# Layer two's projection: each head's reciprocal norm is copied over its 16 rows by DMA instead of by a matrix product

## The chip, the core and the metric

The kernel runs as one program on one core of a Trainium2 chip. The metric is the time of one execution on the device in microseconds (us). The engines named below are TensorE (PE; its weight loads are PEld), VectorE (DVE), ScalarE (ACT), GpSimd (POOL) and SyncE (SP), which here only issues DMA transfers and waits.

## The reference, cut to what matters

Two transformer-like layers run over 2 x 2048 tokens of width 256 with 16 heads of 16 columns. The change lies in layer two, between its layer norm and its attention:

```python
def _l2norm(t):
    n = jnp.sqrt(jnp.sum(t * t, axis=-1, keepdims=True))
    return t / jnp.maximum(n, EPS)
def heads(W):                      # x is the layer-normed input, (B, T, 256)
    y = jnp.einsum('btd,od->bto', x, W)
    return y.reshape(B, T, NUM_HEADS, HEAD_DIM).transpose(0, 2, 1, 3)
Q = _l2norm(heads(Wq))
K = _l2norm(heads(Wk))
V = heads(Wv)
cos_sim = jnp.clip(jnp.einsum('bhtd,bhsd->bhts', Q, K), -0.999, 0.999)
```

So every 16 values of a query or key head are multiplied by one number, the reciprocal of their norm. The attention that follows (an arccos, a 16th power, a normalised product with V), the output projection and a feed-forward branch are the same in both kernels.

## The kernel before

The program is a row of phases, each of them a block that all engines leave together: constants; then for each layer the weights, the layer norm, the projection, the attention and the output. The phase of this study is the projection of layer two (`projection_phase` with `L == 1`, prefix `p1`).

It works on 8 blocks (`TB`) of 512 tokens. The normed input `xTa` lies transposed (features on partitions). In a block there are four feature tiles `ft` of 128 rows, two of queries and two of keys; a tile holds 8 heads of 16 rows (`FH` = 8, `DH` = 16). For each block:

- PE computes the values of two 128-token tiles (L528), then for each `ft` the projection `psS[ft % 2]` (L547) and behind it the product `expand` of the block before (L537), then the other two tiles of values, then `norms` (L520). `norms` adds the squares of each head: the 8 sums of tile `ft` land on partitions 32*ft to 32*ft+7 of `psO[0]`.
- ACT copies the values out (L570), copies each projection to `proj` (L584) and squares it to `sq` (L586), and takes the reciprocal root of the norms, `n_sb` (L599).
- DVE limits that to `r_norm` (L657) and then, for each `ft`, waits for `expand`, multiplies `proj` by it (L660) and splits the result into three bf16 parts that sum to it (`split_parts`, L437 to L440).
- SP stores the three parts of each `ft` to `qk_parts` in device memory (L487, 384 KB, rows of 1 KB) and the block's values to `v_store` (L491). The whole of `xTa` goes to `xT_store` in one transfer of 4 MB at the phase's start (L483).

`expand` is what puts a head's number on its 16 rows: a product of `r_norm` (8 rows used of 32) with the constant 0/1 matrix `selT`.

What sets the order is semaphores. DVE's `r_norm` waits for L599, which waits for `norms`, the last product of its block. `parts` has two buffers, so the split of a tile waits until the store of the tile two before it has landed (`s_st`). `proj` has two buffers (`projs`), so ACT's copy waits for the splits of two blocks before. DVE and ACT run a loop of two blocks; PE's program is written out.

Layer one's projection (`L == 0`) has the same shape without `expand`. In it SP also stores the bf16 parts of the norms: per block four transfers of 24 KB to `norm_parts` (L496), each out of 8 partitions that begin at partition 0, 32, 64 or 96:

```python
for f in range(NQK):
    sp.dma_start(io["norm_parts"][:, f * FH:(f + 1) * FH, bass.ds(i * 512, 512)]
                 .rearrange("a p t -> p a t"), n_parts[f * NCOL:f * NCOL + FH]).then_inc(s_nst, 16)
```

Of the kernel before, what the change touches and what calls it, by code (L numbers as in the profile page):

```python
# [13 lines left out]
F32 = mybir.dt.float32  # L14
BF16 = mybir.dt.bfloat16
ALU = mybir.AluOpType
# [36 lines left out]
class Mem:  # L53


    def __init__(self, nc, ctx):
# [28 lines left out]
        self.sels = self.q_stack[1][:, :].bitcast(F32)[:, 0:P + NCOL]  # L85
# [74 lines left out]
def load_projection(sp, m, io, L, loaded):  # L160

    vg_w = 2 * D if L == 0 else D
    sp.dma_start(m.wqk, io[f"wqk{L}"].rearrange("(k p) n -> p k n", p=P)).then_inc(loaded, 16)
    sp.dma_start(m.wvg[:, 0:KD * vg_w].rearrange("p (k n) -> p k n", k=KD),
                 io[f"wvg{L}"].rearrange("(k p) n -> p k n", p=P)).then_inc(loaded, 16)
    sp.dma_start(m.sels[:, 0:NCOL], io["sel"]).then_inc(loaded, 16)
    sp.dma_start(m.sels[:, NCOL:NCOL + P], io["selT"]).then_inc(loaded, 16)
    return 64
# [274 lines left out]
def projection_phase(nc, m, io, L):  # L443
# [3 lines left out]
    pre = f"p{L}"  # L447
    xTa = m.area(2 * NT * D, KD, B * T)
    vg_w = 2 * D if L == 0 else D
# [6 lines left out]
    selT = m.sels[:, NCOL:NCOL + P]  # L456
# [8 lines left out]
    r_norm = m.area(11520, 512)  # L465
    n_loads = 2
    with ExitStack() as ctx:
        (s_load, s_dve, s_bias, s_bias_row, s_proj, s_P, s_sq, s_nm, s_nsb, s_nparts, s_nst, s_vps, s_vfree, s_rn,
         s_e, s_efree, s_parts, s_v) = sems(
            nc, ctx, pre, "load", "dve", "bias", "bias_rows", "proj", "projected", "squared", "norm_mm", "norm_copied",  # L470
            "norm_parts", "norm_stored", "v_ready", "v_free", "rnorm", "expanded", "expand_free", "parts",
            "values")
        s_st = sems(nc, ctx, pre, "stored0", "stored1")
        s_xT, s_vst, s_ones = sems(nc, ctx, pre, "xT_stored", "values_stored", "stack_ones")
# [3 lines left out]
        def _(sp):  # L478
            if L == 0:
                sp.dma_start(bqk, io["bqk"]).then_inc(s_load, 16)  # L480
                sp.dma_start(bvg[0:1, :], io["bvg"]).then_inc(s_load, 16)
            if L == 1:
                sp.dma_start(io["xT_store"], xTa).then_inc(s_xT, 16)  # L483
            with sp.Fori(0, TB) as i:
                for ft in range(NQK):
                    sp.wait_ge(s_parts, 4 * i + ft + 9)
                    sp.dma_start(io["qk_parts"][:, ft * P:(ft + 1) * P, bass.ds(i * 512, 512)]  # L487
                                 .rearrange("a p t -> p a t"), parts[ft % 2]).then_inc(s_st[ft % 2], 16)
                if L == 1:
                    sp.wait_ge(s_vfree, 4 * i + 6)  # L490
                    sp.dma_start(io["v_store"][:, bass.ds(4 * i, 4), :], m.values[:, bass.ds(4 * i, 4), :])\  # L491
                        .then_inc(s_vst, 16)
                if L == 0:
                    sp.wait_ge(s_nparts, i + 2)
                    for f in range(NQK):
                        sp.dma_start(io["norm_parts"][:, f * FH:(f + 1) * FH, bass.ds(i * 512, 512)]  # L496
                                     .rearrange("a p t -> p a t"), n_parts[f * NCOL:f * NCOL + FH]).then_inc(s_nst, 16)
            for x in s_st:
                sp.wait_ge(x, 16 * (2 * TB + 1))
            if L == 1:  # L500
                sp.wait_ge(s_xT, 16)
                sp.wait_ge(s_vst, 16 * TB)
            if L == 0:
                sp.wait_ge(s_nst, 16 * (NQK * TB + 1))

        @block.tensor
        def _(pe):
            pe.sem_inc(s_nm, 1)
            if L == 0:
                pe.wait_ge(s_load, 16 * n_loads)  # L510
                nc.tensor.matmul(m.psM[0][:, :], m.ones_row[0:1, :], bvg[0:1, :], start=True, stop=True)\
                    .then_inc(s_bias_row, 1)
                pe.wait_ge(s_bias, 2)
# [18 lines left out]
            def expand(i, ft):  # L532

                pe.wait_ge(s_rn, i + 2)
                pe.wait_ge(s_efree, 4 * i + ft + 1)
                rows = slice(ft * NCOL, (ft + 1) * NCOL)
                nc.tensor.matmul(m.psS[ft % 2][:, 512:1024], selT[rows, :], r_norm[rows, :], start=True, stop=True)\  # L537
                    .then_inc(s_e, 1)


            for i in range(TB):
                if L == 1:
                    values(i, range(2))
                for ft in range(NQK):
# [5 lines left out]
                    if L == 0:  # L550
                        values(i, (ft,))
                    elif i > 0:
                        expand(i - 1, ft)
                if L == 1:
                    values(i, (2, 3))
                norms(i)
            if L == 1:
                for ft in range(NQK):
                    expand(TB - 1, ft)

        @block.scalar
        def _(act):
            act.sem_inc(s_P, 2)
            act.sem_inc(s_nsb, 1)
            if L == 0:
                act.wait_ge(s_bias, 2)
            def act_block(i, proj):
                def value_tile(tt):
                    act.wait_ge(s_vps, 4 * i + tt + 1)
                    nc.scalar.activation(m.values[:, bass.ds(4 * i + tt, 1), :], m.psM[tt % 2][:, 0:D].unsqueeze(1),  # L570
                                         ACT.Copy).then_inc(s_vfree, 1)

                if L == 1:
                    for tt in range(2):
                        value_tile(tt)
                act.wait_ge(s_nm, i + 1)
                for ft in range(NQK):
                    act.wait_ge(s_proj, 4 * i + ft + 1)
                    act.wait_ge(s_parts, 4 * i + ft + 1)
                    if L == 0:  # L580
                        nc.scalar.activation(proj[:, ft, :], m.psS[ft % 2][:, 0:512], ACT.Identity,
                                             bias=bqk[:, ft:ft + 1], scale=-2.0 if ft < 2 else 1.0).then_inc(s_P, 1)
                    else:
                        nc.scalar.activation(proj[:, ft, :], m.psS[ft % 2][:, 0:512], ACT.Copy).then_inc(s_P, 1)  # L584
                    act.wait_ge(s_P, 4 * i + ft + 3)
                    nc.scalar.activation(sq[:, ft, :], proj[:, ft, :], ACT.Square,  # L586
                                         scale=0.5 if L == 0 and ft < 2 else 1.0).then_inc(s_sq, 1)
                if L == 1:
                    value_tile(2)
                    value_tile(3)  # L590
                act.wait_ge(s_nm, i + 2)
                if L == 0:
                    act.wait_ge(s_nparts, i + 1)
                else:
                    act.wait_ge(s_rn, i + 1)
                if L == 0:
                    nc.scalar.activation(n_sb, m.psO[0][:, :], ACT.Copy).then_inc(s_nsb, 1)
                else:
                    nc.scalar.activation(n_sb, m.psO[0][:, :], ACT.Abs_reciprocal_sqrt, bias=ZERO_SHIFT)\  # L599
                        .then_inc(s_nsb, 1)  # L600
# [6 lines left out]
        def _(dve):  # L607
            dve.sem_inc(s_parts, 8)
            dve.sem_inc(s_vfree, 2)
            dve.sem_inc(s_efree, 2)  # L610
            dve.sem_inc(s_nparts, 1)
            dve.sem_inc(s_rn, 1)
# [3 lines left out]
            per_block = NQK * 3 + (3 if L == 0 else 0)  # L616
            chain_n = [0]
            if L == 0:
                dve.wait_ge(s_load, 16 * n_loads)
                nc.vector.tensor_scalar(bqk[:, 0:2], bqk[:, 0:2], -2.0, None, ALU.mult).then_inc(s_bias, 1)  # L620
                dve.wait_ge(s_bias_row, 1)
                nc.vector.tensor_copy(bvg_all, m.psM[0][:, :]).then_inc(s_bias, 1)
                dve.wait_ge(s_bias, 2)
            def dve_block(i, proj):
# [21 lines left out]
                if L == 0:  # L646
                    for ft in range(NQK):
                        dve.wait_ge(s_P, 4 * i + ft + 3)
                        split(ft)
                        value_tile(ft)  # L650
                    dve.wait_ge(s_nsb, i + 2)
                    dve.wait_ge(s_nst, 16 * NQK * i + 16)
                    split_parts(nc, link, n_sb, n_parts, n_rest).then_inc(s_nparts, 1)
                else:
                    dve.wait_ge(s_nsb, i + 2)

                    nc.vector.tensor_scalar(r_norm, n_sb, 1.0 / NORM_EPS, None, ALU.min).then_inc(s_rn, 1)  # L657
                    for ft in range(NQK):
                        dve.wait_ge(s_e, 4 * i + ft + 1)
                        nc.vector.tensor_tensor(proj[:, ft, :], m.psS[ft % 2][:, 512:1024], proj[:, ft, :], ALU.mult)\  # L660
                            .then_inc(s_efree, 1)
                        dve.wait_ge(s_efree, 4 * i + ft + 3)
                        split(ft)
# [5 lines left out]
        if L == 0:  # L669
            @block.gpsimd  # L670
            def _(pool):
                pool.wait_ge(s_proj, NQK * TB)
                pool.wait_ge(s_vps, NQK * TB)
                pool.wait_ge(s_nm, TB + 1)
                for stack in m.q_stack + m.k_stack:
                    nc.gpsimd.memset(stack[ROWS:P, :], 1.0).then_inc(s_ones, 1)
                pool.wait_ge(s_ones, 2 * B)
# [725 lines left out]
def program(nc, ins, out):  # L1403
    with ExitStack() as ctx:
# [11 lines left out]
        for L in range(2):  # L1416
# [4 lines left out]
            projection_phase(nc, m, mine, L)  # L1421
            if L == 0:
                distance_phase(nc, m, mine)
            else:
                cosine_phase(nc, m, mine)
# [3 lines left out]
def layout(inputs):  # L1429
# [21 lines left out]
        "ident": np.eye(P, dtype=np.float32), "sel": sel, "selT": np.tile(sel.T, (NQK, 1)),  # L1451
# [16 lines left out]
```

## Time and profile before

| | us |
|---|---|
| median of 3 runs | 7010.25 (7005.66 to 7014.32) |
| the profiled execution | 7006.62 |
| its span, first to last instruction | 7004.8 |
| layer two's projection in it, from PE's first product to DVE's last split | 2554.8 to 2698.9 |

The profile is one execution. "Busy" is the time in which an engine executes; the granted clock of PE is given as a share of full speed; the share of DMA is the mean busy share of the core's 16 DMA engines. A row of a timeline gives the start, the length, the engine, the source line and what was written from what; in brackets stands how long the engine had been idle and what ended that. SPq is the queue on which SyncE issues transfers.

### The profile page before, as it was taken

The page shows a single profiled execution, that of the slowest core. Times are in us where ns is not written, and L with a number is a line of the kernel's source. Part 1 is how long each engine was busy: PE and PEld are TensorE (multiplying, and loading weights), DVE is VectorE, ACT ScalarE, POOL GpSimd, SP SyncE. Part 2 cuts the span into 40 slices and gives each one's busy share as a digit, 9 for nine tenths or more (in the row PEclk, how much of TensorE's full clock was granted, in tenths as well). Part 3 has the DMA queues.
Part 4 walks back from the last instruction along what each step waited for, and adds up shares of the span by engine and source line. Part 5 has one row for each costly group of instructions (what it writes and reads, how often), then busy time and mean ns, then how long its engine had stood idle before and what let it go on. Part 6 is the DMA issues. An engine that isn't in the chain of part 4 may idle for free. (4 is left out here: it accounts for less than half of the span.)

```text
span 7004.8 us, 55795 instructions
## 1 busy us (share of the span) xinstructions
PE 4109.5 (59%) x17200; PEld 1398.6 (20%) x17200; DVE 6627.5 (95%) x6134; ACT 6429.7 (92%) x3748; POOL 3427.1 (49%) x1422
## 2 busy tenths in 40 slices
PE   5677777776777675454554554554544555544555
PEld 3222222222222242021111111111211111111212
DVE  7899999999999967999999999999999999999995
ACT  3699999999999935999999999999999999999995
POOL 0244444444444401565655656556565555656553
PEclk8988888889898887555556555565655555565657
DMA  3100000000000042000000000000000000000002
GB/s 130 55 16 12 15 12 16 11 16 14 13 15 12 10 148 72 6 15 8 15 8 9 8 15 8 8 15 8 15 8 9 15 9 8 8 15 8 15 6 98
DMA packets 238807, 157.46 MB, mean 22 GB/s; under 512 B 148798, under 2 KB 222425, under 8 KB 237226
## 3 DMA queue, kind: packets, MB, share of 16 engines
q1 hardware_dynamic: 234474, 151.13, 7.7%
q10 hardware_dynamic: 4160, 4.19, 0.2%
q8 instruction: 88, 1.44, 0.1%
q14 instruction: 85, 0.70, 0.0%
HBM read 95.74 MB, written 59.51 MB: 22 GB/s over the span
## 5 line engine op out<-in xcount | busy, mean ns | idle before, releaser
L1281 POOL TENSOR_TENSOR work<-work 128x1776 f32<-128x1776 f32 (+2 forms) x696 | 2150.9, 3090 | 55.3
L1074 PE MATMUL psS<-q_stack,k_stack 96*128 96x512 bf16 x2048 | 1034.0, 613 | 1675.4 <-DVE work L1190 1613.3
L750 POOL TENSOR_SCALAR work<-work 128x2048 f32<-128x2048 f32 x512 | 970.9, 1896 | 1219.2 <-DVE work L952 1198.2
L1185 DVE TENSOR_SCALAR work<-psS 128x1024 f32<-128x1024 f32 x1024 | 1204.9, 1218 | 77.0 <-PE psS L1074 54.0
L1278 POOL TENSOR_SCALAR work<-work 128x1776 f32<-128x1776 f32 (+2 forms) x174 | 286.5, 1647 | 1988.3 <-ACT work L1165 1980.9
L940 DVE SCALAR_TENSOR_TENSOR work<-work,psS 128x1024 f32<-128x1024 f32 x1024 | 1216.9, 1212 | 43.4 <-ACT work L899 43.4
L899 ACT ACTIVATE work<-psS 128x1024 f32<-128x1024 f32 x1024 | 1160.2, 1133 | 48.2 <-PE psS L768 47.9
L1190 DVE TENSOR_TENSOR work<-psS,work 128x1024 f32<-128x1024 f32 x1024 | 1200.3, 1213 | 0.0
L1196 DVE SCALAR_TENSOR_TENSOR work<-work 128x2048 f32<-128x2048 f32 x512 | 1141.6, 2284 | 35.0 <-ACT work L1161 35.0
L768 PE MATMUL psS<-q_stack,k_stack 102*128 102x512 bf16 x2048 | 703.9, 430 | 660.0 <-DVE work L940 625.3
L914 ACT ACTIVATE work<-work 128x2048 f32<-128x2048 f32 x512 | 1035.8, 2023 | 2.8 <-POOL work L750 2.8
L1157 ACT ACTIVATE work<-work 128x2048 f32<-128x2048 f32 (+2 forms) x259 | 912.3, 3565 | 83.8 <-DVE work L1190 82.0
L952 DVE TENSOR_TENSOR work<-work 128x1632 f32<-128x1632 f32 x512 | 950.4, 1857 | 0.3 <-ACT work L914 0.3
L1165 ACT ACTIVATE work<-work 128x6144 f32<-128x6144 f32 (+2 forms) x174 | 907.9, 5218 | 27.2 <-DVE work L1196 27.2
L1161 ACT ACTIVATE work<-work 128x2048 f32<-128x2048 f32 (+1 forms) x343 | 915.9, 2740 | 1.0
L1092 PE MATMUL psO<-work,v_tile 128*32 128x512 f32 x4096 | 649.2, 799 | 396.2 <-issue 344.4
L786 PE MATMUL psO<-work,v_tile 128*32 128x512 f32 x4096 | 658.1, 720 | 6.9 <-DVE work L952 4.8
L1074 PEld LDWEIGHTS psS<-q_stack,k_stack 96*128 96x128 bf16 x2048 | 142.1, 111 | 2526.2 <-DVE work L1190 2382.8
L1170 ACT ACTIVATE work<-work 128x3888 f32<-128x3888 f32 (+2 forms) x174 | 578.8, 3374 | 1.0
L1174 ACT ACTIVATE work<-work 128x3888 f32<-128x3888 f32 (+2 forms) x174 | 577.4, 3365 | 0.0
L768 PEld LDWEIGHTS psS<-q_stack,k_stack 102*128 102x128 bf16 x2048 | 134.0, 100 | 1389.1 <-DVE work L940 1350.0
L1207 DVE TENSOR_TENSOR work<-work 128x480 f32<-128x480 f32 (+2 forms) x696 | 407.0, 653 | 0.0
(141 smaller groups left out, 3950.4 us busy)
## 6 DMA issues: line engine op xcount, KB each, us to landing
qk_parts<-work SPq DMA_DIRECT2D x64, 384.0 KB, 3.2
q_stack<-qk_parts SPq DMA_DIRECT2D x384, 64.0 KB, 2.3
k_stack<-qk_parts SPq DMA_DIRECT2D x384, 64.0 KB, 2.3
xT_store<-work SPq DMA_DIRECT2D x2, 4096.0 KB, 16.5
ffn_in<-xT_store SPq DMA_DIRECT2D x64, 128.0 KB, 2.5
work<-in_x SPq DMA_DIRECT2D x1, 4096.0 KB, 14.3
xn_store<-work SPq DMA_DIRECT2D x1, 4096.0 KB, 13.1
work<-xn_store SPq DMA_DIRECT2D x4, 1024.0 KB, 11.8
```

Of the source, the lines that this page charges most:

```text
L750: nc.gpsimd.tensor_scalar(slot, slot, F32_MAX, 0.0, ALU.min, ALU.max).then_inc(s_m, 1)
L899: nc.scalar.activation(ring[:, u % RING, half * 1024:(half + 1) * 1024], m.psS[half][:, :], ACT.Abs_reciprocal_sqrt, bias=ZERO_SHIFT)\
L914: nc.scalar.activation(slot, slot, ACT.Abs_reciprocal_sqrt, bias=SHEP_EPS * SHEP_EPS, scale=2 * SHEP_EPS).then_inc(s_v, 1)
L940: nc.vector.scalar_tensor_tensor(part, part, 0.5 / SHEP_EPS, m.psS[half][:, :], ALU.add, ALU.mult).then_inc(s_y, 1)
L952: nc.vector.tensor_tensor(part, part, part, ALU.mult).then_inc(s_wd, 1)
L1074: last = nc.tensor.matmul(m.psS[half][:, q * 512:(q + 1) * 512], m.k_stack[b][0:ROWS, kt * P:(kt + 1) * P], m.q_stack[b][0:ROWS, c:c + 512 ...
L1157: nc.scalar.activation(square(p, size), square(p, size), ACT.Ln, bias=1.0, scale=-1.0)\
L1161: nc.scalar.activation(square(p, size), square(p, size), ACT.Sigmoid, scale=-0.5)\
L1185: nc.vector.tensor_scalar(cosine(j, p)[:, 0, cols], m.psS[half][:, :], COS_MAX, -COS_MAX, ALU.min, ALU.max).then_inc(s_cl, 1)
L1190: nc.vector.tensor_tensor(square(p)[:, 0, cols], m.psS[half][:, :], cosine(j, p)[:, 0, cols], ALU.mult).then_inc(s_q, 1)
L1196: nc.vector.scalar_tensor_tensor(cosine(j, p), square(p), RSIN_MAX, cosine(j, p), ALU.min, ALU.mult).then_inc(s_z, 1)
L1281: nc.gpsimd.tensor_tensor(part, part, part, ALU.mult).then_inc(s_pp, 1)
```

## The change

The projection of layer two gets a function of its own, `cosine_projection_phase`; `projection_phase` keeps layer one's part with nothing in it changed, and the constant `selT` with its load is gone. In the new function:

- `expand` is gone. For each block SP issues four transfers from SBUF to SBUF, which copy each of the 8 rows of `r_norm` of a tile to 16 partitions (`r_all`, 256 KB for each tile, rows of 2 KB). DVE multiplies by `r_all`.
- DVE limits the norms of block `i` and then works on block `i - 1`. `projs` has three buffers, `r_norm` and `r_all` have two.
- `xT_store` is written in 8 slices, one with each block's values, behind that block's four copies.
- The loops are written out, and the table for L599's function is loaded once ahead of them.

```diff
-            def expand(i, ft):
-                pe.wait_ge(s_rn, i + 2)
-                pe.wait_ge(s_efree, 4 * i + ft + 1)
-                rows = slice(ft * NCOL, (ft + 1) * NCOL)
-                nc.tensor.matmul(m.psS[ft % 2][:, 512:1024], selT[rows, :], r_norm[rows, :], start=True, stop=True)\
-                    .then_inc(s_e, 1)
...
-                sp.dma_start(io["xT_store"], xTa).then_inc(s_xT, 16)
...
+def cosine_projection_phase(nc, m, io):
...
+    projs = [m.area(at, NQK, 512) for at in (4096, 12288, 4 * NT * D)]
...
+    r_norm = [m.area(10240 + 512 * i, 512) for i in range(2)]
+    r_all = [m.area(2048 * i, NQK, 512) for i in range(2)]
...
+        @block.sync
+        def _(sp):
+            for i in range(TB + 1):
+                if i < TB:
+                    sp.wait_ge(s_rn, i + 1)
+                    if i >= 2:
+                        sp.wait_ge(s_unit, NQK * (i - 1))
+                    for ft in range(NQK):
+                        rows = r_norm[i % 2][ft * NCOL:ft * NCOL + FH, :]
+                        sp.dma_start(r_all[i % 2][:, ft, :], rows.unsqueeze(1).broadcast_to([FH, DH, 512]))\
+                            .then_inc(s_all[i % 2], 16)
+                    tok = slice(i * 512, (i + 1) * 512)
+                    sp.wait_ge(s_vfree, 4 * i + 4)
+                    sp.dma_start(io["v_store"][:, 4 * i:4 * i + 4, :], m.values[:, 4 * i:4 * i + 4, :]).then_inc(s_vst, 16)
+                    sp.dma_start(io["xT_store"][:, :, tok], xTa[:, :, tok]).then_inc(s_xT, 16)
+                if i > 0:
+                    tok = slice((i - 1) * 512, i * 512)
+                    for ft in range(NQK):
+                        sp.wait_ge(s_parts, NQK * (i - 1) + ft + 1)
+                        sp.dma_start(io["qk_parts"][:, ft * P:(ft + 1) * P, tok].rearrange("a p t -> p a t"),
+                                     parts[ft % 2]).then_inc(s_st[ft % 2], 16)
...
+        @block.scalar
+        def _(act):
...
+                for ft in range(NQK):
+                    act.wait_ge(s_proj, NQK * i + ft + 1)
+                    if i >= 3:
+                        act.wait_ge(s_parts, NQK * (i - 3) + ft + 1)
+                    nc.scalar.activation(proj[:, ft, :], m.psS[ft % 2][:, 0:512], ACT.Copy).then_inc(s_P, 1)
...
+        @block.vector
+        def _(dve):
+            link = Chain(dve, s_split)
+            for i in range(TB + 1):
+                if i < TB:
+                    dve.wait_ge(s_nsb, i + 1)
+                    nc.vector.tensor_scalar(r_norm[i % 2], n_sb, 1.0 / NORM_EPS, None, ALU.min).then_inc(s_rn, 1)
+                if i > 0:
+                    proj = projs[(i - 1) % 3]
+                    spread = r_all[(i - 1) % 2]
+                    dve.wait_ge(s_all[(i - 1) % 2], 16 * NQK * ((i - 1) // 2 + 1))
+                    for ft in range(NQK):
+                        n = NQK * (i - 1) + ft
+                        dve.wait_ge(s_P, n + 1)
+                        dve.wait_ge(s_sq, n + 1)
+                        nc.vector.tensor_tensor(proj[:, ft, :], spread[:, ft, :], proj[:, ft, :], ALU.mult)\
+                            .then_inc(s_unit, 1)
+                        dve.wait_ge(s_unit, n + 1)
+                        if n >= 2:
+                            dve.wait_ge(s_st[ft % 2], 16 * (n // 2))
+                        split_parts(nc, link, proj[:, ft, :], parts[ft % 2], rest).then_inc(s_parts, 1)
+                        dve.wait_ge(s_parts, n + 1)
```

## Rows read from the trace of the kernel before

**Rows 1.** Busy time of each engine, granted clock and DMA in three stretches.

```profile
core 0: us, PE busy (x) PEld busy (x) DVE busy (x) ACT busy (x) POOL busy (x), PEclk, DMA share, GB/s
2554.80:2699.00 144.20, 133.23 (x384) 57.50 (x384) 97.17 (x168) 65.66 (x112) 0.00 (x0) 0.95 0.40 139
2569.60:2586.10 16.50, 16.50 (x49) 7.00 (x48) 12.51 (x22) 7.18 (x14) 0.00 (x0) 1.00 0.21 72
...
2690.00:2699.00 9.00, 2.04 (x2) 0.49 (x2) 8.31 (x15) 0.00 (x0) 0.00 (x0) 0.50 0.39 131
```

**Rows 2.** Groups by line, 2545 to 2705 us: busy, mean ns, idle before, its releaser.

```profile
L547 PE MATMUL psS<-work,k_stack 128*128 128x512 f32 x128 | 61.8, 609 | 0.0
L537 PE MATMUL psS<-work,q_stack 32*128 32x512 f32 x64 | 35.8, 655 | 4.4 <-DVE work L660 2.9 <-DVE work L657 1.5
...
L660 DVE TENSOR_TENSOR work<-psS,work 128x512 f32<-128x512 f32 x32 | 22.1, 691 | 24.0 <-PE psS L537 22.5
...
L657 DVE TENSOR_SCALAR work<-work 128x512 f32<-128x512 f32 x8 | 3.4, 427 | 21.0 <-ACT work L599 20.5
```

**Rows 3.** Timeline, DVE and PE in the first block that has a predecessor.

```profile
2569.53 0.43 DVE L657 TENSOR_SCALAR work<-work 128x512 f32<-128x512 f32 x1 [18.66 <-ACT work L599]
...
2572.80 0.69 DVE L660 TENSOR_TENSOR work<-psS,work 128x512 f32<-128x512 f32 x1 [2.83 <-PE psS L537]
...
2573.63 0.43 DVE L437 CAST work<-work 128x512 bf16<-128x512 f32 x1
...
2575.28 0.69 DVE L440 TENSOR_TENSOR work<-work 128x512 bf16<-128x512 f32 x1
...
2585.59 0.43 DVE L657 TENSOR_SCALAR work<-work 128x512 f32<-128x512 f32 x1
```

**Rows 4.** Timeline, the first block, in which PE has no `expand`.

```profile
2558.31 7.03 PE L547 MATMUL psS<-work,k_stack 128*128 128x512 f32 x16
...
2567.61 1.28 ACT L599 ACT_TABLE_LOAD   x1
...
2569.83 1.88 PE L547 MATMUL psS<-work,k_stack 128*128 128x512 f32 x4
```

**Rows 5.** Timeline, the end of the phase and the first transfer of the next.

```profile
2698.18 0.69 DVE L440 TENSOR_TENSOR work<-work 128x512 bf16<-128x512 f32 x1
...
2699.70 0.36 SPq L491 DMA_DIRECT2D v_store<-work  x1
2706.51 2.66 SPq L1042 DMA_DIRECT2D q_stack<-qk_parts  x6
```

**Rows 6.** DMA issues, 2545 to 2720 us: KB each, median us from issue to landing.

```profile
qk_parts<-work SPq DMA_DIRECT2D x32, 384.0 KB, 3.2
xT_store<-work SPq DMA_DIRECT2D x1, 4096.0 KB, 13.0
v_store<-work SPq DMA_DIRECT2D x8, 512.0 KB, 3.6
```

**Rows 7.** SP's timeline in layer one's projection: four `norm_parts` stores.

```profile
188.23 1.74 SPq L496 DMA_DIRECT2D norm_parts<-work  x4
```

**Rows 8.** DMA totals, 188.9 to 191.1 us: those four stores and nothing else.

```profile
DMA packets 128, 0.10 MB, mean 45 GB/s; under 512 B 32, under 2 KB 128, under 8 KB 128
...
q1 hardware_dynamic: 128, 0.10, 28.4%
```

**Rows 9.** DMA totals, 191.6 to 193.1 us: one `qk_parts` store of 384 KB.

```profile
DMA packets 392, 0.39 MB, mean 257 GB/s; under 512 B 16, under 2 KB 392, under 8 KB 392
...
q1 hardware_dynamic: 392, 0.39, 77.9%
```

**Rows 10.** Stretches as in Rows 1, cut small, during the four `norm_parts` stores.

```profile
188.90:189.00 0.10, 0.10 (x1) 0.00 (x0) 0.10 (x1) 0.00 (x0) 0.00 (x0) 1.00 0.00 0
189.10:189.20 0.10, 0.10 (x2) 0.09 (x1) 0.10 (x1) 0.00 (x0) 0.00 (x0) 1.00 0.48 61
...
190.10:190.20 0.10, 0.10 (x2) 0.06 (x1) 0.10 (x1) 0.10 (x1) 0.00 (x0) 1.00 0.49 61
...
188.90:190.90 2.00, 2.00 (x6) 0.83 (x5) 1.68 (x4) 1.32 (x2) 0.00 (x0) 1.00 0.31 49
```

More of the change, by code:

```diff
@@ L165, in load_projection @@
                  io[f"wvg{L}"].rearrange("(k p) n -> p k n", p=P)).then_inc(loaded, 16)
-    sp.dma_start(m.sels[:, 0:NCOL], io["sel"]).then_inc(loaded, 16)
-    sp.dma_start(m.sels[:, NCOL:NCOL + P], io["selT"]).then_inc(loaded, 16)
-    return 64
+    sp.dma_start(m.sels, io["sel"]).then_inc(loaded, 16)
+    return 48
 def constants_phase(nc, m, io):
@@ L440, in split_parts, with projection_phase @@
     return nc.vector.tensor_tensor(parts[:, 2, :], rest, parts[:, 1, :], ALU.subtract)
-def projection_phase(nc, m, io, L):
-    pre = f"p{L}"
+def projection_phase(nc, m, io):
+    pre = "p0"
     xTa = m.area(2 * NT * D, KD, B * T)
-    vg_w = 2 * D if L == 0 else D
+    vg_w = 2 * D
     wqk = m.wqk
@@ L455, in projection_phase @@
     sel = m.sels[:, 0:NCOL]
-    selT = m.sels[:, NCOL:NCOL + P]
     projs = [m.area(at, NQK, 512) for at in (4096, 12288)]
@@ L464, in projection_phase @@
     n_parts = m.work[:, 10752:11520].bitcast(BF16).rearrange("p (a t) -> p a t", a=3)
-    r_norm = m.area(11520, 512)
     n_loads = 2
     with ExitStack() as ctx:
-        (s_load, s_dve, s_bias, s_bias_row, s_proj, s_P, s_sq, s_nm, s_nsb, s_nparts, s_nst, s_vps, s_vfree, s_rn,
-         s_e, s_efree, s_parts, s_v) = sems(
+        (s_load, s_dve, s_bias, s_bias_row, s_proj, s_P, s_sq, s_nm, s_nsb, s_nparts, s_nst, s_vps, s_vfree, s_parts,
+         s_v) = sems(
             nc, ctx, pre, "load", "dve", "bias", "bias_rows", "proj", "projected", "squared", "norm_mm", "norm_copied",
-            "norm_parts", "norm_stored", "v_ready", "v_free", "rnorm", "expanded", "expand_free", "parts",
-            "values")
+            "norm_parts", "norm_stored", "v_ready", "v_free", "parts", "values")
         s_st = sems(nc, ctx, pre, "stored0", "stored1")
-        s_xT, s_vst, s_ones = sems(nc, ctx, pre, "xT_stored", "values_stored", "stack_ones")
+        (s_ones,) = sems(nc, ctx, pre, "stack_ones")
         block = ctx.enter_context(nc.Block())
@@ L478, in _ @@
         def _(sp):
[L479 to L482, printed above, removed]
-                sp.dma_start(io["xT_store"], xTa).then_inc(s_xT, 16)
+            sp.dma_start(bqk, io["bqk"]).then_inc(s_load, 16)
+            sp.dma_start(bvg[0:1, :], io["bvg"]).then_inc(s_load, 16)
             with sp.Fori(0, TB) as i:
@@ L488, in _ @@
                                  .rearrange("a p t -> p a t"), parts[ft % 2]).then_inc(s_st[ft % 2], 16)
[L489 to L497, printed above, removed]
+                sp.wait_ge(s_nparts, i + 2)
+                for f in range(NQK):
+                    sp.dma_start(io["norm_parts"][:, f * FH:(f + 1) * FH, bass.ds(i * 512, 512)]
+                                 .rearrange("a p t -> p a t"), n_parts[f * NCOL:f * NCOL + FH]).then_inc(s_nst, 16)
             for x in s_st:
                 sp.wait_ge(x, 16 * (2 * TB + 1))
[L500 to L504, printed above, removed]
+            sp.wait_ge(s_nst, 16 * (NQK * TB + 1))
         @block.tensor
@@ L508, in _ @@
             pe.sem_inc(s_nm, 1)
[L509 to L513, printed above, removed]
+            pe.wait_ge(s_load, 16 * n_loads)
+            nc.tensor.matmul(m.psM[0][:, :], m.ones_row[0:1, :], bvg[0:1, :], start=True, stop=True)\
+                .then_inc(s_bias_row, 1)
+            pe.wait_ge(s_bias, 2)
             def norms(i):
@@ L549, in _ @@
                     last.then_inc(s_proj, 1)
[L550 to L555, printed above, removed]
+                    values(i, (ft,))
                 norms(i)
-            if L == 1:
-                for ft in range(NQK):
-                    expand(TB - 1, ft)
         @block.scalar
@@ L564, in _ @@
             act.sem_inc(s_nsb, 1)
-            if L == 0:
-                act.wait_ge(s_bias, 2)
+            act.wait_ge(s_bias, 2)
             def act_block(i, proj):
[L568 to L575, printed above, removed]
                 act.wait_ge(s_nm, i + 1)
@@ L579, in act_block @@
                     act.wait_ge(s_parts, 4 * i + ft + 1)
[L580 to L584, printed above, removed]
+                    nc.scalar.activation(proj[:, ft, :], m.psS[ft % 2][:, 0:512], ACT.Identity,
+                                         bias=bqk[:, ft:ft + 1], scale=-2.0 if ft < 2 else 1.0).then_inc(s_P, 1)
                     act.wait_ge(s_P, 4 * i + ft + 3)
                     nc.scalar.activation(sq[:, ft, :], proj[:, ft, :], ACT.Square,
[L587 to L590, printed above, removed]
+                                         scale=0.5 if ft < 2 else 1.0).then_inc(s_sq, 1)
                 act.wait_ge(s_nm, i + 2)
[L592 to L600, printed above, removed]
+                act.wait_ge(s_nparts, i + 1)
+                nc.scalar.activation(n_sb, m.psO[0][:, :], ACT.Copy).then_inc(s_nsb, 1)
             with act.Fori(0, TB // 2) as ii:
@@ L609, in _ @@
             dve.sem_inc(s_vfree, 2)
-            dve.sem_inc(s_efree, 2)
             dve.sem_inc(s_nparts, 1)
-            dve.sem_inc(s_rn, 1)
             for x in s_st + [s_nst]:
                 dve.sem_inc(x, 16)
-            per_block = NQK * 3 + (3 if L == 0 else 0)
+            per_block = NQK * 3 + 3
             chain_n = [0]
[L618 to L623, printed above, removed]
+            dve.wait_ge(s_load, 16 * n_loads)
+            nc.vector.tensor_scalar(bqk[:, 0:2], bqk[:, 0:2], -2.0, None, ALU.mult).then_inc(s_bias, 1)
+            dve.wait_ge(s_bias_row, 1)
+            nc.vector.tensor_copy(bvg_all, m.psM[0][:, :]).then_inc(s_bias, 1)
+            dve.wait_ge(s_bias, 2)
             def dve_block(i, proj):
@@ L644, in value_tile @@
                         .then_inc(s_vfree, 1)
[L646 to L663, printed above, removed]
+                for ft in range(NQK):
+                    dve.wait_ge(s_P, 4 * i + ft + 3)
+                    split(ft)
+                    value_tile(ft)
+                dve.wait_ge(s_nsb, i + 2)
+                dve.wait_ge(s_nst, 16 * NQK * i + 16)
+                split_parts(nc, link, n_sb, n_parts, n_rest).then_inc(s_nparts, 1)
             with dve.Fori(0, TB // 2) as ii:
@@ L667, in _ @@
                     dve_block(2 * ii + par, projs[par])
[L669 to L677, printed above, removed]
+        @block.gpsimd
+        def _(pool):
+            pool.wait_ge(s_proj, NQK * TB)
+            pool.wait_ge(s_vps, NQK * TB)
+            pool.wait_ge(s_nm, TB + 1)
+            for stack in m.q_stack + m.k_stack:
+                nc.gpsimd.memset(stack[ROWS:P, :], 1.0).then_inc(s_ones, 1)
+            pool.wait_ge(s_ones, 2 * B)
@@ L1450, in layout @@
         "b2": a["L1_ffn_b2"].reshape(1, D),
-        "ident": np.eye(P, dtype=np.float32), "sel": sel, "selT": np.tile(sel.T, (NQK, 1)),
+        "ident": np.eye(P, dtype=np.float32), "sel": sel,
     }
```

75 lines of the change are left out of this document (71 added, 4 removed).

## The prediction

> **What bounds the phase now.** I read the stretches first. From 2569.6 to 2586.1 us, one block of 16.5 us, PE is busy for 16.50 us at a granted clock of 1.00, while DVE works 12.5 us and ACT 7.2 us; over the whole phase PE is busy 133 of 144 us [rows 1]. So PE's list of products sets the pace. The groups by line say the same from DVE's side: its multiplication L660 idled 22.5 us for `expand` (L537), and L657 idled 20.5 us for the norms, 18.7 of it once, at the start [rows 2, 3]. `expand` holds 35.8 us of PE [rows 2]. The timeline gives its true price: a block without it takes PE from 2558.31 to 2569.83, 11.5 us [rows 4], against 16.5 us with it [rows 1], so 5.0 us a block.
>
> DVE is the next bound. From one L660 at 2572.80 to the L657 behind four tiles at 2585.59 is 12.8 us, or 3.2 us a tile, of which the split takes 2.45 us (2573.63 to the end of L440 at 2575.97, and a gap of 0.1) [rows 3]. With L657 (0.43 us [rows 2] and a gap) a block costs DVE 13.3 us.
>
> Then I read the transfers, because the change puts its work there. A `qk_parts` store lands 3.2 us after its issue, `v_store` 3.6, the whole `xT_store` 13.0 [rows 6]. I split the 3.2 us in three. Nothing moves for 0.8 us (SP issues at 188.23 and the share is still 0.00 until 189.0 [rows 7, 10]). The data takes 1.25 us: 77.9% of 16 engines for 1.5 us is 18.7 us of packets, so 50 ns per KB on one engine and 1.2 us on sixteen [rows 9]. The remaining 1.1 us pass until the semaphore counts.
>
> **The change part by part.**
>
> *`expand` removed, DVE one block behind.* PE falls to 11.5 us a block, below DVE's 13.3. DVE's multiplication now reads two tiles in SBUF; L440 does that with the same size in 0.69 us, and L660 takes 0.69 [rows 3], so nothing changes there. If nothing else came in, the phase would go at DVE's pace. The first `r_norm` would come at 2568.3 (2569.53 less the table load of 1.28 in front of it [rows 3, 4], since the table is now loaded ahead), the second 11.5 us later and a little more, at 2580.4. Block 0 then takes 0.5 + 12.8, six blocks 13.3 each, the last 12.8: the end is at 2686.3 instead of 2698.9 [rows 5], which is 12.6 us earlier.
>
> *The four copies.* They move 256 KB each, 1 MB a block, and each reads only 8 partitions. Layer one's `norm_parts` stores read 8 partitions at the same four places, so they are the nearest rows. Two things show there. Four transfers leave 32 small packets, 8 each, where a store from 128 partitions leaves 16 [rows 8, 9]; these mark the engines that took part, so half the engines carry such a transfer. And these engines are slow: 28.4% of 16 for 2.2 us is 10.0 us for 96 KB, 104 ns per KB where the wide store needs 50 [rows 8, 9]. In the tenths of a microsecond in which all eight are busy (a share of 0.48 or 0.49), they move 61 GB/s together; over two microseconds it is 49 GB/s, or 51 without the first empty tenth [rows 10]. The reason must be the source, since a `qk_parts` store writes the same kind of rows to the same memory at 50 ns. A copy of 262,144 bytes therefore takes 4.3 us at 61 GB/s and 5.1 us at 51. I take the middle, 4.7 us, and 18.8 us for a block's four, since all four use the same eight engines one after the other.
>
> The bounds below that: 3.3 us if the mean of 104 ns per KB holds (32 KB for each of eight engines); 1.6 us if the engines don't hinder each other (50 ns); 0.8 us if also all sixteen take part.
>
> The Trainium skill says both things as rules. "DMA: Bandwidth & Descriptors", section on why a DMA increments its semaphore by 16: the engines used are the largest number up to 16 that divides the slowest dimension of both sides, here 8; by this, the trace agrees (8 small packets a transfer). "SBUF — State Buffer", section on the DMA port swizzle: partitions 0 to 3 and 32 to 35 are reached by one port of about 27 GB/s, 4 to 7 and 36 to 39 by another. By that rule 8 partitions give 54 GB/s and a copy 4.85 us, which would make the time 7142.
>
> *Where the copies stand in the queue.* This decides their price. In step `i` SP issues, right behind `r_norm` of block `i`, its four copies, then `v_store` and the slice of `xT_store`, and only then the `qk_parts` stores of block `i - 1`. DVE doesn't wait for its own block's copies, which were issued a step before. But the split of tile 2 waits for the landing of tile 0's store, and this stands behind all of them. Moving `xT_store` into slices adds to that: one slice is an eighth of 13.0 - 1.9, so 1.4 us, and `v_store` 3.6 - 1.9, so 1.7 us [rows 6], together 3.1.
>
> A block then takes, from the end of the last split of the block before: 0.05 until SP issues that tile's store, 0.8 to its data, 1.25 data, 18.8 for the copies, 3.1 for the values and the slice, 1.25 for tile 0's store, 1.1 until it counts, 2.45 for the rest of tile 2 and 3.2 for tile 3. The sum is **32.0 us**, against 16.5. PE works 11.5 of them; should its clock fall to 0.50 as it does where only the tail's few products run [rows 1], it needs 23 and still isn't the bound. The third buffer of `projs` only lets ACT run ahead of a DVE that waits: nothing. The table loads that go, the written-out loops and `selT`'s load lie beside the queue's work: nothing.
>
> *The start.* The first copies are issued at 2568.8 and move from 2569.6 to 2588.4, so DVE begins block 0 at 2589.5. Values and slice of block 0 end at 2591.5, the second copies at 2610.3, values and slice at 2613.4, tile 0's store at 2614.7, and it counts at 2615.8. With 2.45 + 3.2 block 0 ends at 2621.4. Six blocks of 32.0 end at 2813.4, and the last, behind which nothing is queued, takes 12.8: 2826.2. That is 127.3 us later than 2698.9.
>
> *The end.* Before, the last transfer was `v_store`, issued at 2699.70, landing 3.6 later, 4.4 us behind DVE [rows 5, 6]. Now it is a `qk_parts` store, 0.2 + 3.2 = 3.4 us behind: 1.0 us less.
>
> **Sum.** The profiled execution took 7006.6 (span 7004.8), and 7006.6 + 127.3 - 1.0 = 7132.9. The median of before lies 3.6 us higher, so I predict **7137 us**, 1.8% slower. Each 0.1 us on a copy is 3.2 us on the whole (four copies, eight times in the chain): 7124 at 4.3 us, 7150 at 5.1.
>
> **Rivals.**
>
> *Copies of 3.3 us* (the eight engines hinder each other only half of the time, as their mean packet says). For it: the 104 ns are a mean over real transfers. Against it: those had 24 KB each with 0.44 us from issue to issue [rows 7], so the queue had pauses, and a long copy has none. A block takes 26.4 us, and four copies of 1.4 us less count eight times (twice at the start, six blocks), 44.8 us: 7092.
>
> *Copies of 1.6 us* (only the halved number of engines costs). A block takes 19.6 us; block 0 ends at 2599.5, the phase at 2729.9: +31 - 1, so 7040. Against it stands the 104 ns.
>
> *All sixteen engines, 0.8 us.* A block 16.4, as long as before; the phase ends at 2707.3: +8.4 - 1, so 7018. Against it stand both readings of rows 8.
>
> *The other side, not slower: the stores don't stand behind the copies.* If packets of different transfers pass each other, or engines idle in a copy carry the stores, DVE never waits, and the phase ends at 2686.3: -12.6 - 1.0, so 6997. It decides only if tile 0's store lands within 7.6 us of the block's end (0.5 + 6.4 + 0.7), while in order it needs 7.55 us even with copies of no length. With all in one queue the phase breaks even at copies of about 0.55 us, and that would be 480 GB/s, more than the 320 of a wide store (384 KB in 1.2 us [rows 9]). For it: 1 MB of copies, 1 MB of values and slice and 1.5 MB of parts take a free queue only some 11 us of 13.3.
>
> **Chances and range.** Copies of 4.3 to 5.1 us 0.60; of 3.3 us 0.14; of 1.6 us 0.09; sixteen engines 0.06; hidden 0.08; longer than 5.1 us 0.03. A measurement of this kernel tells 0.2%, 14 us, from no change. Sixteen engines is no change; hidden is 13.6 us, on that line, and I give 0.05 of it to faster and the rest to the same side: faster 0.05, same 0.10, slower 0.85. The range goes from 7030, which takes in the 1.6 us, to 7160, above the 7150 of the longest copy; it leaves out 0.17. The likeliest case alone lies between 7115 and 7155.
>
> **What the new profile would show.** Copies landing some 6 us after issue when alone, and the fourth some 20; DMA share about 0.4 to 0.5 during them, at 50 to 60 GB/s; DVE idle about 18 us once a block, at the first cast (L437) of tile 2, released by a `qk_parts` store and not by the copies; PE idle for over half of the phase and its clock down; the phase 270 us long. I am wrong if the copies go at over 100 GB/s, or if DVE's idle time stands at the multiplication instead, or if the tile 0 stores land within 8 us.

## The result, and the profile after

The changed kernel took 7155.63, 7156.43 and 7162.72 us, median 7156.43 (a fourth run, of 9427 us, was disturbed and is left out; with it the median is 7159.58), against a median of 7008.65 us for the kernel before, which by now has a fourth run too. The ratio is 1.021, 95% interval 1.019 to 1.023: the change makes the kernel 2.1% slower. I had forecast 7137 us and a range from 7030 to 7160, so the result lies in the range, but at its upper end and above the 7115 to 7155 of my likeliest case.

DVE's waits in the phase of the changed kernel (line waited for: us in total, times, longest):

```profile
DVE work L436 <- DMA qk_parts<-work: 149.3, 7, 22.0
DVE work L731 <- DMA work<-work: 13.0, 1, 13.0
```

L436 is the first cast of a split; L731 is the multiplication, which waits for the copies. Before, DVE waited 22.5 us at the multiplication, and for PE [rows 2]. Now it stands 21.3 us (mean) in each of seven steps at the split of tile 2, for a store, and only once for a copy. Rows of DVE's and SP's timeline, from the phase's start, one block and the phase's end:

```profile
2596.37 0.69 DVE L731 TENSOR_TENSOR work<-work 128x512 f32<-128x512 f32 x1 [12.97 <-DMA work<-work]
...
2627.98 0.43 DVE L722 TENSOR_SCALAR work<-work 128x512 f32<-128x512 f32 x1
...
2656.61 0.43 DVE L436 CAST work<-work 128x512 bf16<-128x512 f32 x1 [21.40 <-DMA qk_parts<-work]
...
2662.09 0.43 DVE L722 TENSOR_SCALAR work<-work 128x512 f32<-128x512 f32 x1
...
2845.95 0.69 DVE L439 TENSOR_TENSOR work<-work 128x512 bf16<-128x512 f32 x1
2852.01 2.67 SPq L1102 DMA_DIRECT2D q_stack<-qk_parts  x6
```

A block lasts 34.1 us here (from one L722, the instruction that limits the norms, to the next) and 34.4 in the mean of six. The same block on SP's queue:

```profile
2628.46 10.21 SPq L641 DMA_DIRECT2D work<-work  x4
2638.72 4.25 SPq L645 DMA_DIRECT2D v_store<-work  x1
2643.01 5.58 SPq L646 DMA_DIRECT2D xT_store<-work  x1
2648.63 13.82 SPq L651 DMA_DIRECT2D qk_parts<-work  x4
```

SP doesn't only queue the transfers, it is held up while it issues them: the four copies take it 10.2 us, the values 4.25 (0.36 in the kernel before [rows 5]) and the slice 5.6, so that it issues tile 0's store, ready at about 2631.4, at 2648.6. The store lands 7.9 us later. Stretches of the same block show the rate:

```profile
2632.00:2636.00 4.00, 4.00 (x14) 2.54 (x13) 3.04 (x6) 1.10 (x3) 0.00 (x0) 0.93 0.45 49
...
2641.00:2643.00 2.00, 1.46 (x7) 0.95 (x5) 0.00 (x0) 0.00 (x0) 0.00 (x0) 1.00 0.46 50
2643.00:2645.00 2.00, 0.00 (x0) 0.00 (x0) 0.00 (x0) 0.00 (x0) 0.00 (x0) 1.00 0.82 153
...
2648.00:2652.00 4.00, 0.00 (x0) 0.00 (x0) 0.00 (x0) 0.00 (x0) 0.00 (x0) 0.50 0.65 113
```

In the first two stretches only copies are under way: the share is 0.45 to 0.46, about half of the engines, and they move 49 to 50 GB/s, as the `norm_parts` stores did over two microseconds [rows 10]. In the third, packets of the values pass beside them, on which more below. In the last stretch PE and DVE both stand idle; PE last worked until 2642.5, and its granted clock is 0.50, which is 1.2 GHz.

### The profile page after: what moved, and what is told of

Read it like the earlier page. It is cut to its first block and busy times, and to the rows that moved or that the text cites. A ratio compares the mean times of both kernels' runs of the same rounds, so it can differ in the third digit from the quotient of the medians.

```text
span 7154.6 us, 55226 instructions
## 1 busy us (share of the span) xinstructions
PE 4068.5 (57%) x17136; PEld 1397.8 (20%) x17136; DVE 6628.3 (93%) x6134; ACT 6422.8 (90%) x3741; POOL 3429.2 (48%) x1422
## 5 line engine op out<-in xcount | busy, mean ns | idle before, releaser
L1152 PE MATMUL psO<-work,v_tile 128*32 128x512 f32 x4096 | 646.9, 797 | 396.7 <-issue 344.7
L846 PE MATMUL psO<-work,v_tile 128*32 128x512 f32 x4096 | 638.5, 700 | 6.9 <-DVE work L1012 4.8
## 6 DMA issues: line engine op xcount, KB each, us to landing
work<-in_x SPq DMA_DIRECT2D x1, 4096.0 KB, 14.3
```

## The experiments

The comparisons are with runs of the kernel before on the same chips (medians of 7011.7 to 7013.1 us). A time without an interval is that of a single run. A block's length is DVE's, the mean from one L722 (or what stands in its place) to the next over the phase.

**The copies left out.**

```diff
-                    for ft in range(NQK):
-                        rows = r_norm[i % 2][ft * NCOL:ft * NCOL + FH, :]
-                        sp.dma_start(r_all[i % 2][:, ft, :], rows...).then_inc(s_all[i % 2], 16)
-                    dve.wait_ge(s_all[(i - 1) % 2], 16 * NQK * ((i - 1) // 2 + 1))
-                    spread = r_all[(i - 1) % 2]
+                    spread = fill                 # 128 x 2048, set once to 0.1
```

> Leaves the four copies out: DVE multiplies by a constant tile of 0.1 that it fills once, so q and k aren't normalised. Everything else is as in the changed kernel. If the copies are what stalls the phase (my theory), the waits of the first cast of tile 2 on a store shrink from about 21 us to under 2 us, a block takes 13.3 to 14.2 us, and the time is 6997 to 7003 us. Rival: the values and the slice of xT_store ahead of the stores, or a PE clock that falls because PE pauses, cost the time; then a block stays over 16.5 us and the time is 7010 or more.

Measured: 6991.67 us, ratio 0.997 (0.996 to 0.998). The waits for stores are gone:

```profile
DVE work L436 <- DMA qk_parts<-work: 0.2, 1, 0.2
```

A block takes 12.8 us, less than the 13.3 that I had counted, and the time is below the 6997 to 7003 expected. So the slices and the values cost nothing while no copies are in the queue, and without the copies the change would gain 21 us. (That a slice costs time behind copies is measured below. PE's clock isn't what costs it: DVE's waits are for stores, and in the changed kernel PE works only 103 of the phase's 289 us.)

**The same bytes from other rows.** Three kernels change only what a copy reads.

```diff
-                        rows = r_norm[i % 2][ft * NCOL:ft * NCOL + FH, :]
+                        (wide)      source fill[:, ft, :], no repetition
+                        (apart)     rows = fill[0:32:4, ft, :]
+                        (adjacent)  rows = fill[0:8, ft, :]
```

> The four transfers keep their size, destination, place in the queue and semaphores, but each reads 128 partitions of a constant tile (0.1) in place of 8 rows 16 times over; q and k aren't normalised. Theory (the narrow source is slow): a transfer takes about 0.8 us of the queue, a block 16.4 us, the time is about 7018 us. Rival (a transfer from SBUF to SBUF of 256 KB is slow by itself, or 2 KB rows are): it stays near 5 us, a block near 34 us, the time near 7156.

> The copies read 8 rows 16 times over as in the changed kernel, but rows of a constant tile (0.1) that lie 4 partitions apart (0, 4, ... 28) in place of 8 adjacent ones; q and k aren't normalised. Theory (adjacent partitions share a way out of SBUF, and the eight engines stand in line at it): each engine is then alone, a copy takes about 1.6 us, a block 19.6 us, the time is about 7040 us. Rival (eight engines, or reading one row again and again, are slow wherever the rows lie): a copy stays near 5 us, the time near 7156.

> The control of the runs with the constant tile: 8 adjacent rows (partitions 0 to 7) of it, copied 16 times over, for all four feature tiles; q and k aren't normalised. Theory: as the changed kernel, a copy about 5 us, a block 34 us, 7150 to 7162 us. If instead it were the fresh r_norm, written by DVE just before, that makes the copies slow, this one would come out below 7100.

Measured: 7010.58, 7035.77 and 7147.11 us. Stretches in which only copies are under way (after the granted clock stand the share of DMA and GB/s), of the wide source:

```profile
2610.50:2613.50 3.00, 3.00 (x18) 1.66 (x17) 2.83 (x6) 2.13 (x5) 0.00 (x0) 1.00 0.93 323
```

of the rows 4 apart:

```profile
2602.50:2605.00 2.50, 2.50 (x17) 1.82 (x10) 2.36 (x5) 0.99 (x3) 0.00 (x0) 1.00 0.53 151
```

and of the adjacent rows:

```profile
2628.00:2634.00 6.00, 6.00 (x17) 3.59 (x16) 3.09 (x6) 2.00 (x5) 0.00 (x0) 0.83 0.46 51
```

The last two have the same size, destination and repetition, both keep about half of the engines busy, and they differ in the distance of the rows: 151 against 51 GB/s, so a copy of 262,144 bytes takes 1.7 or 5.1 us. Blocks take 15.5, 18.8 and 33.2 us. The first two times are below what was expected (by 7 and 4 us), and so is the third, by 3; it is far above 7100, so that r_norm is fresh isn't what makes the copies slow.

**More rows to read.** The norms' product computes 32 rows for each tile and uses 8. With a constant that gives each head's sum on four of them, a copy reads 32 rows.

```diff
+    "sel4": np.repeat(sel[:, 0:FH], 4, axis=1)     # loaded for layer two in place of sel
-                        rows = r_norm[i % 2][ft * NCOL:ft * NCOL + FH, :]
-                        ... rows.unsqueeze(1).broadcast_to([FH, DH, 512])
+                        rows = r_norm[i % 2][ft * NCOL:(ft + 1) * NCOL, :]
+                        ... rows.unsqueeze(1).broadcast_to([NCOL, 4, 512])
```

> As the changed kernel, with its order, but the norms' product uses a constant whose 32 columns give each head's sum four times (at no cost to PE, which computed 32 rows anyway), so that each copy reads 32 adjacent rows 4 times over in place of 8 rows 16 times. If the number of separate places in SBUF that a copy reads is what counts (8 groups of four, as in the run with rows 4 apart), a copy takes 1.2 to 1.7 us and the time is 7024 to 7036 us. If the number of engines counts (now sixteen), a copy takes 0.8 us as from 128 rows and the time is 7011 us. If repeated reading of a row is slow, it stays above 7050.

Measured: 7033.28 us, a block 18.4 us, and during the copies:

```profile
2601.00:2604.00 3.00, 3.00 (x19) 1.65 (x18) 2.83 (x6) 2.07 (x5) 0.00 (x0) 1.00 1.03 207
```

Now all engines are busy, and still they move 207 GB/s and not 323. Over eight groups of four adjacent rows that is 26 GB/s a group; the changed kernel's copies read two groups at 50 GB/s, so 25 each. With rows 4 apart there are eight groups too, but eight engines at a share of 0.53 move 151, 19 each, about what an engine moves in the wide transfer (323 / 16 = 20). So two limits act: what an engine moves (about 20 GB/s) where there are groups enough, and what a group gives (25 to 26) where there aren't. The runs alone leave the size of a group open between four and eight rows: groups of eight that give 50 fit all four kernels too. Groups of two would give the rows 4 apart at most 8 x 12.5 = 100 GB/s, and they got 151; groups of sixteen would give 32 rows 100, and they got 207. That four adjacent rows are the unit is the Trainium skill's rule ("SBUF — State Buffer", the DMA port swizzle: one port of about 27 GB/s for them); the traces agree with it, with 25 and 26.

**The order in the queue.**

```diff
                 for ft in range(NQK):
+                    ... store of block i - 1, tile ft
+                    ... copy of block i, tile ft
+                ... v_store, slice of xT_store
-                ... four copies, v_store, slice of xT_store, then the stores
```

> The same transfers as in the changed kernel in another order: in each step SP issues store, copy, store, copy, store, copy, store, copy, and the values and the slice of xT_store last. A copy still takes 5.1 us. Theory (each transfer stands behind those issued before it): the store of tile 0 now lands in time, and DVE waits at the multiplication, for the last copy of its block, in place of the cast; a block takes about 30.4 us in place of 34.3, the time is about 7130 us. Rival (the place in the queue doesn't matter, the engines share their time over all that is issued): the block stays at 34 us, the time near 7156.

Measured: 7127.31 us, a block 30.4 us, and the wait has moved:

```profile
DVE work L732 <- DMA work<-work: 114.1, 8, 15.1
...
DVE work L436 <- DMA qk_parts<-work: 20.5, 7, 3.2
```

L732 is the multiplication. The place in the queue decides which wait it is; by my estimate the queue's content is still about 29 us a block (four copies at 5.2, four stores at 1.25, 3.1 for values and slice).

**The slice of xT_store.**

```diff
+            sp.dma_start(io["xT_store"], xTa).then_inc(s_xT, 16)      # once, ahead of the loop
-                    sp.dma_start(io["xT_store"][:, :, tok], xTa[:, :, tok]).then_inc(s_xT, 16)
```

> The changed kernel, but xT_store goes out whole at the phase's start, as in the kernel before, in place of a slice behind each block's copies. Theory: each slice stood for 1.4 us between the copies and tile 0's store, eight times; a block takes 32.9 in place of 34.3 us and the time is about 7145 us. Rival: a slice costs more than its share of the data, because it is split in 2 KB rows and meets the copies of the next tiles; a block falls to 32 us or less, the time to 7138 or less. Rival: it passes the copies on the engines that these don't use and costs nothing; 7156.

Measured: 7145.45 us, a block 32.7 us: a slice stands for 1.7 us a block, near the 1.4 that I had priced.

**The copies on ACT's queue.**

```diff
+                act.wait_ge(s_rn, i + 1)          # behind L714, in ACT's program
+                ... the same four copies with act.dma_start
```

> The changed kernel's copies, issued by ACT on its own queue right behind its reciprocal root, in place of SP. A copy still takes 5.1 us. Theory: the two queues share the engines, so a store no longer stands behind all copies; but the eight engines still have 20.4 us of copies and 8 us of their part of the other transfers to carry in each block, 28.5 us in all, and DVE waits at the multiplication for the copies; the time is about 7110 us. Rival: the engines carry stores while a copy's packets wait for their rows, so only the copies' 20.4 us count and the time is about 7050. Rival: the queue of issue makes no difference; 7156.

Measured: 7106.10 us. The time and the block (28.9 us) are close to the first theory's 7110 and 28.5; its place for the wait is wrong:

```profile
DVE work L436 <- DMA qk_parts<-work: 110.2, 14, 15.7
```

DVE waits for stores still, now twice a block. Two of a block's four stores are issued while the copies run on the other queue, and they land 19 to 20 us after their issue; the other two land after 3.2 to 3.4 us. So stores share engines with the copies and are slow beside them. SP isn't held up any more (the values take it 0.49 us to issue). A queue of their own takes the copies out of SP's way; the length of the block fits the 28.5 us that I had estimated for the busier engines.

**Two versions without the stall.** The first takes the copies from 32 rows, `xT_store` whole, and a step's order copy, copy, store, copy, store, copy, store, values, store. The second has neither copies nor `expand`; it too has `xT_store` whole and the values ahead of tile 3's store:

```diff
+    "ones16": np.kron(np.eye(FH), np.ones((DH, DH)))                  # 128 x 128
-                    last = nc.tensor.matmul(m.psO[0][f * NCOL:(f + 1) * NCOL, :], sel, sq[:, f, :], ...)
+                    nc.tensor.matmul(norm_ps[f], m.ones16, sq[:, f, :], ...)      # four PSUM banks
-                nc.scalar.activation(n_sb, m.psO[0][:, :], ACT.Abs_reciprocal_sqrt, ...)
+                    nc.scalar.activation(r_all[i % 2][:, f, :], norm_ps[f], ACT.Abs_reciprocal_sqrt, ...)
-                        nc.vector.tensor_tensor(proj[:, ft, :], spread[:, ft, :], proj[:, ft, :], ALU.mult)
+                        nc.vector.scalar_tensor_tensor(proj[:, ft, :], spread[:, ft, :], 1.0 / NORM_EPS,
+                                                       proj[:, ft, :], ALU.min, ALU.mult)
```

> The copies from 32 rows, and the queue put in order: xT_store whole at the phase's start as in the kernel before, and in each step copy, copy, store, copy, store, copy, store, values, store. Theory: no stall is left, DVE sets the pace with 12.8 us a block, and the time is that of the run without copies, 6990 to 6997 us, 0.3% below the kernel before. Rival: the queue holds 11 to 13 us of transfers a block, too close to DVE's 12.8; stores come late by 1 to 2 us, and the time is 7000 to 7012.

> No copies and no second product: the norms' product itself uses a 128 x 128 constant with a block of 16 x 16 ones for each head, so that each head's sum comes out on all its 16 rows; ACT takes the reciprocal root tile by tile into r_all, and DVE limits and multiplies in one instruction. PE takes 13.9 us a block (11.5 less 1.06 for the old norms, plus four products of 0.86), DVE 12.4, ACT about 9. The time is 6985 to 6997 us. Rival: ACT's four roots behind the last product of a block delay PE's next block, which then takes over 15 us, and the time is 7002 or more.

Measured: 6992.85 us, ratio 0.9973 (0.9963 to 0.9984), and 6988.11 us, ratio 0.9968 (0.9957 to 0.9979), both 0.3% below the kernel before and clear of the noise. One hundred microseconds of each, 2580 to 2680; first the 32 rows:

```profile
2580.00:2680.00 100.00, 68.30 (x238) 36.16 (x236) 92.57 (x162) 41.62 (x78) 0.00 (x0) 0.86 0.83 229
```

then the ones product:

```profile
2580.00:2680.00 100.00, 87.03 (x253) 47.72 (x252) 83.17 (x143) 55.99 (x103) 0.00 (x0) 0.96 0.44 152
```

In the first DVE sets the pace: a block takes 13.0 us, DVE's waits for stores are down to 2.4 us in the whole phase, and the DMA share is 0.83. In the second PE sets it: a block takes 13.75 us, PE has no pause from 2560 to 2680, and the DMA share is about half of the first's. The two intervals overlap, so that no difference between them is shown. I would keep the second, since it leaves the queue the most room.

## Why the prediction came out as it did

*PE and DVE.* This was right. PE no longer bounds the phase, and a block costs DVE 12.8 us where I had 13.3, since r_norm's instruction overlaps the next multiplication (0.34 us from start to start). The multiplication out of SBUF takes 0.69 us, as before.

*The number of engines and the rate.* The mechanism was right: the share of 0.45 and the 49 to 50 GB/s have their forerunners in the shares of 0.48 and 0.49 and in the 51 GB/s of [rows 10]. I took the middle between 61 and 51 GB/s, 4.7 us a copy, where a copy alone takes 5.1 to 5.4 us. The estimate of 4.85 us from the figure of the Trainium skill ("SBUF — State Buffer", the DMA port swizzle) was closer and still short. Rows 8 and 10 hold short transfers with pauses, and their best tenths of a microsecond aren't what a long one sustains.

*The chain of a block.* I summed 32.0 us, and the mean is 34.4. The step that was mis-sized is the copies' 18.8 us. In the block shown, of 34.1 us, their packets run for 22.5 us, 5.6 us a copy, which is the case that I had given a chance of 0.03. Two other errors lie in the same sum: the first cast of tile 2 follows 4.1 us behind the copies' last packet where I had 3.1 + 1.25 + 1.1 = 5.45 us, and the rest takes 5.5 us in place of 5.65. So 3.7 us too few on the copies were in part made up for by 1.5 us too many elsewhere.

At 50 GB/s the copies' 1 MB would take 21 us. The other 1.5 us come from what meets them. Counted in the trace, 24 or 25 packets of the copies begin in each microsecond while they are alone, and one takes 0.30 us (a packet of the slice, of 2 KB too, takes 0.08). From 2643 to 2646 packets of the values (4 KB each, 58 of them until 2645) pass beside them, and from 2649 to 2651 those of the slice: then 13 to 19 packets of the copies begin in each microsecond, and one takes up to 0.57 us. The values' 58 packets are 119 of the 153 GB/s in the stretch shown above, so the copies fell from 50 to 34 GB/s. In the control with adjacent rows at partitions 0 to 7 for all tiles the values pass beside the third and fourth copy just the same, and these aren't slowed: of these 169 GB/s the values' 57 packets are 117, the copies 52.

```profile
2640.00:2642.00 2.00, 0.00 (x0) 0.00 (x0) 0.00 (x0) 0.00 (x0) 0.00 (x0) 1.00 0.76 169
```

Its four copies run for 21.1 to 21.9 us, and its blocks are 1.2 us shorter. In the changed kernel the third copy, which reads from partition 64 on, begins at 2640.5 and goes at 50 GB/s until the values arrive (2641 to 2643 above). So neither the place of the rows nor the company alone slows it, but both together. The control's rows are of another tensor too, and which partitions the passing packets read isn't in the trace, so why the two meet stays open. By this passing half of the values (64 of 128 packets) and some of the slice get done while the copies run, which is my explanation, not tested by itself, of why the 5.45 us shrank to 4.1.

*The start.* DVE began block 0 at 2596.37, 38.8 us into the phase; I had 34.7. The first four copies took 24.5 us from issue to use in place of 20.7, the same term again; `r_norm` came 0.4 us later than I had it.

*The sum.* From PE's first product to DVE's last split the phase took 144.1 us before and 289.1 after (2557.55 to 2846.64), 145.0 more where I had 127.3: 14.3 from six blocks, 3.8 from the start up to block 0's end, -0.4 from the last. The end gave back 2.3 us (5.4 us from DVE to the next phase's first transfer, 7.6 before) where I had 1.0. The rest of the span's 149.8 lies where nothing was changed: 2.8 ahead of the phase and 4.3 behind it. The run without copies has 1.0 and 2.5 there, so part of that is what differs from one execution to the next. No run explains the rest, and my sum had no term for it: it had 7132.9 us for an execution that took 7156.43. Of these 23.5 us, 17.7 lie in the phase, -1.3 at its end, and 7.1 are these.

That the time stayed inside the range, by 3.6 us, is partly luck. The range's upper end had been set 10 us above the time of the slowest copy that I had counted, without a reason of its own.

*The rivals.* Three of the four came out as an experiment of their own: 16 engines 7018, measured 7011; 1.6 us a copy 7040, measured 7036; nothing queued in the way 6997, measured 6992. The first two hold for sources which this kernel doesn't have, and the third for a queue without copies. Copies of 3.3 us had no experiment; the 5.1 to 5.4 us measured rule them out. The rival that stores pass the copies fails: with copies first DVE waits for stores, with stores first for copies.

*The signs.* DVE's wait, its place and its releaser came as forecast (18 us a block, measured 21.3), and so did the DMA share; the rate lies at the lower edge of the 50 to 60 GB/s, and the phase took 289 us and not 270. One sign was badly chosen. I would be wrong, I wrote, if tile 0's stores landed within 8 us, and they do land 7.7 to 8.2 us after their issue. But SP issues them some 17 us late; from when its data is ready the store in the block shown takes 25 us. I hadn't foreseen that part of the wait would pass on SP, ahead of the queue.

*PE's clock.* As said, it fell to 0.50 inside a block, after PE had stopped for lack of work. It didn't bound the phase: in all of it PE was busy for 103 of 289 us.

```profile
2557.55:2846.64 289.09, 102.96 (x320) 53.28 (x320) 96.61 (x168) 56.16 (x105) 0.00 (x0) 0.68 0.48 100
```

## What to carry to other kernels

Price a transfer by the rows that it reads as well as by its bytes: look in the trace for any transfer out of as few partitions, however small, and take its lowest sustained rate, not its best moment. Then write down everything that one queue issues between the event and the landing that somebody waits for, and ask what passes beside the slow transfer; a buffer that was free in time before (`parts`, two deep) is where the wait comes back. And where a product already computes rows that nobody uses, let it compute the copies.

## What the runs showed of the hardware

Eight adjacent partitions gave 49 to 51 GB/s in every case here, read once (`norm_parts`) or 16 times over and from two different tensors, eight rows 4 partitions apart 151, thirty-two adjacent ones 207, a hundred and twenty-eight 323. I had expected the first from the trace; that 16 engines can be busy to a share of 1.03 and deliver 207 GB/s I had not. A busy share of the DMA engines says how long packets take, not how much they carry: 0.46 meant 50 GB/s from adjacent rows and 0.53 meant 151 from rows apart.

I also had not expected the issuing engine to be held: SP took 10.2 us to issue four copies of adjacent rows, 2.5 us from 128 partitions, and 3.5 us with rows 4 apart:

```profile
2600.36 3.50 SPq L644 DMA_DIRECT2D work<-work  x4
```

So a slow transfer also delays what its engine would do next. And it can be slowed itself by packets that pass beside it: 24 or 25 of its packets in a microsecond became 13 to 19.
